# Moving the rounding of two more chunks of h from VectorE to ScalarE in the early blocks of a routed expert network

## The chip, the cores and the metric

The kernel runs on one core of a Trainium2 chip. The metric is the device time of one execution in microseconds, the median of several runs.

## The reference

Each of 32 samples (256 rows of 256 values) is scaled by its condition vector, multiplied by a weight and normalised; the result goes through a mixture of eight experts, of which each row takes the best two, and is added to x.

```python
ys = y * scale
d = rsqrt(einsum('bi,io->bo', ys * ys, weight * weight) + EPS)
z = einsum('bsi,io->bso', x * ys[:, None, :], weight) * d[:, None, :]
logits = einsum('bsd,de->bse', z, Wr) + br
# softmax, top 2 of 8, the two weights normalised: routed
h = relu(einsum('bsd,edh->ebsh', z, W1) + b1)          # 256 -> 1024
expert_out = einsum('ebsh,ehd->ebsd', h, W2) + b2      # 1024 -> 256
out = x + einsum('bse,ebsd->bsd', routed, expert_out)
```

## The kernel before

**Stages.** Stage A computes z and the routing of the first half of the rows. Stage B then works through blocks of rows that share an expert: 14 early blocks (N1 = 14, written out one by one, rows of the first half only), then a loop over further full blocks up to number 38 (NA), then tail blocks of 256 rows. Early and full blocks have 384 rows in three tiles of 128. While the early blocks run, the routing of the second half of the rows is computed in small pieces between their steps (`second_half` on VectorE, ScalarE and TensorE).

**Precision.** TensorE multiplies in fp32r, a rounded form of fp32. Each fp32 operand a is split into a_hi (rounded) and a_lo = a - a_hi, and each product is three matmuls: hi with hi, lo with hi, hi with lo. The split is done for z (z_hi on ScalarE, z_lo on VectorE), for the weights (w_hi on ScalarE, line 783; w_lo on VectorE, line 1396) and for h.

**One block.** The hidden dimension of 1024 is cut into eight chunks c = 0 to 7 of 128. For each chunk:

- `first_product(c)` on TensorE (lines 1653 to 1655): six matmuls of 384 columns into one of two PSUM banks `h_ps[c % 2]`. It waits until ScalarE has read the bank for chunk c - 2.
- ScalarE (`block_of_act`) reads that bank and writes h = relu(. + b1) into one of three SBUF buffers (line 856, counted by `s_relu`). In a chunk that `act_hi` names it first writes h_hi, the rounded relu, from the same bank (line 854, counted by `s_hhi_act`).
- VectorE (`block_of_dve`) makes h_hi from h by a copy (line 1455), unless ScalarE did, and then h_lo = h - h_hi (line 1458, counted by `s_hlo`).
- `second_product(c)` on TensorE (lines 1669 to 1671): nine matmuls of 256 columns, which wait for h_lo.

In the early blocks second products follow three chunks behind. TensorE's order in block b is therefore: first(0), first(1), the six transposes of the next block's rows (line 1631), first(2), first(3), second(0), first(4), second(1), and so on. Between first(1) and first(3) only the transposes and first(2) stand. The wait of a first product is

```python
if not (fresh and c < HP):                 # HP = 2, fresh only in block 0
    pe.wait_ge(s_relu, b * HC + c + 1 - (back(c, HPT) if tail else HP))
```

**ScalarE's order** in an early block: h(0), w_hi of quarter 2, h(1), three copies b2_r (line 864), h(2), w_hi of quarter 3, h_hi(3), h(3), h(4), h(5), w_hi of the next block's quarter 0, h_hi(6), h(6), h_hi(7), h(7), then z_hi and w_hi of the next block's quarter 1. Pieces of the second half's routing stand between some of these in blocks 5 to 10. Instructions of an engine start in this order.

**VectorE's order**: y of the block before, r_cur, then chunk by chunk h_hi (where it is its turn) and h_lo, with w_lo of quarter 2 behind chunk 1, w_lo of quarter 3 behind chunk 3, w_lo of the next block's quarter 0 behind chunk 6, and pieces of the routing behind chunks 2, 4 and 5. first(4) waits for w_lo of quarter 2, first(6) for w_lo of quarter 3.

Of the kernel before, what the change touches and what calls it, by code (L numbers as in the profile page):

```python
# [5 lines left out]
def bass_adaln_moe_ffn(  # L6
# [41 lines left out]
    HC = b1.shape[2]  # L48
# [23 lines left out]
    NHX = 4  # L72
# [22 lines left out]
    N1 = -(-(TOPK * T // 2 - E * (TB - 1)) // TB)  # L95
    NSC1 = N1 * Q
    NB_MIN = NA + -(-(UNITS - Q * NA) // QB)
    ACT_HI = (3, 6, 7)
    TAIL_HI = (3, 6, 7)
    HPT = 3  # L100
    LATE_ACT = (8, 9, 12)
# [13 lines left out]
    with ctx:  # L115
# [3 lines left out]
        def sem(name):  # L119
            return ctx.enter_context(nc.semaphore(name))  # L120
# [258 lines left out]
        s_h2 = sem("s_h2")  # L379
# [12 lines left out]
        def back(c, n=NHP):  # L392

            return n if c >= n else c + 1 + (HC - 1 - c) % n
# [20 lines left out]
        def is_early(b):  # L415
            return isinstance(b, int) and b < N1
# [13 lines left out]
        def act_hi(b, c, tail=False):  # L430
            if tail:
                return c in TAIL_HI
            return isinstance(b, int) and b < N1 - 1 and c in ACT_HI

        def hhi_act(b, c, tail):
            if tail:
                return b * len(TAIL_HI) + (N1 - 1) * len(ACT_HI) - NA * len(TAIL_HI) + TAIL_HI.index(c) + 1
            return b * len(ACT_HI) + ACT_HI.index(c) + 1

        def expert_of(eng, b):  # L440
            if is_early(b):
                eng.wait_ge(s_early, N_EARLY)
                return eng.value_load(early_expert[0:1, b:b + 1], min_val=0, max_val=E - 1)
            if isinstance(b, int):
                eng.wait_ge(s_blocks, N_BLOCKS)
            return eng.value_load(block_expert[0:1, ds(b, 1)], min_val=0, max_val=E - 1)

        def segment_of(eng, b):
            if is_early(b):
                return eng.value_load(early_expert[0:1, b:b + 1], min_val=0, max_val=E - 1)  # L450
            return eng.value_load(block_segment[0:1, ds(b, 1)], min_val=0, max_val=NSEG - 1)
# [250 lines left out]
        def _(act):  # L702
# [76 lines left out]
            def weights_hi(b, k, seg, fresh):  # L779
                act.wait_ge(s_raw[k], seg * 16 + 16)  # L780
                if not fresh:
                    act.wait_ge(s_h2, (b - 1) * HC + (k + 1) * CQ)
                act.activation(w_hi[k][:], raw[k][:], ACT.Copy).then_inc(s_whi, 1)  # L783

            def z_hi_of(b, fresh, width=TB):
                act.wait_ge(s_zt, b + 1)
                if not fresh:
                    act.wait_ge(s_h1, b * HC)
                for c in range(DC):
                    act.activation(z_hi[:, c, 0:width], zt_ps[c][:, 0:width], ACT.Copy).then_inc(s_zhi, 1)  # L790
# [50 lines left out]
            def block_of_act(b, fresh, tail=False):  # L841
                wide = tail or is_early(b)
                width, n_h = (TBT, HPT) if tail else (TB, HP)
                e = expert_of(act, b)
                e_next = expert_of(act, b + 1)
                seg = segment_of(act, b)
                seg_next = segment_of(act, b + 1)
                for c in range(HC):
                    act.wait_ge(s_h1, b * HC + c + 1)
                    if not (fresh and c < NHP):  # L850
                        act.wait_ge(s_hlo, b * HC + c + 1 - back(c))
                    if act_hi(b, c, tail):
                        act.wait_ge(s_h2, b * HC + c + 1 - NHX)
                        act.activation(h_hi[c % NHX][:, 0:width], h_ps[c % n_h][:, 0:width], ACT.Relu,
                                       bias=b1_all[:, ds(e, 1), c]).then_inc(s_hhi_act, 1)
                    act.activation(h[c % NHP][:, 0:width], h_ps[c % n_h][:, 0:width], ACT.Relu,  # L856
                                   bias=b1_all[:, ds(e, 1), c]).then_inc(s_relu, 1)
                    if c == 0:
                        weights_hi(b, 2, seg, fresh)
                    if c == 1:  # L860

                        act.wait_ge(s_rcur, b + 1)
                        for q in range(QB if tail else Q):
                            act.activation(b2_r[:, q, :], b2_all[:, ds(e, 1), :].rearrange("p a d -> p (a d)"),  # L864
                                           ACT.Copy, scale=r_cur[:, q:q + 1]).then_inc(s_b2r, 1)
                    if c == 2:
                        weights_hi(b, 3, seg, fresh)
                    if c == (5 if wide else 4):
                        weights_hi(b + 1, 0, seg_next, False)
                    if c == 5 and not wide:  # L870
                        weights_hi(b + 1, 1, seg_next, False)
                    if is_early(b):
                        second_half(b, c)
                z_hi_of(b + 1, False, width)
                if wide:
                    weights_hi(b + 1, 1, seg_next, False)
# [25 lines left out]
            for b in range(N1):  # L902
                block_of_act(b, b == 0)
            with act.Fori(N1, NA) as b:
                block_of_act(b, False)
            n = blocks_of(act)
            with act.Fori(NA, n) as b:
                block_of_act(b, False, True)
# [837 lines left out]
```

## Time and profile before

| | |
|---|---|
| median of 3 runs | 876.98 us (876.54 to 878.8) |
| profiled execution | 877.7 us, its span 875.9 us |
| TensorE matmuls / weight loads | 842.5 us (96%) / 826.9 us (94%) |
| VectorE | 719.1 us (82%) |
| ScalarE | 563.7 us (64%) |
| GpSimd | 457.5 us (52%) |
| granted TensorE clock, mean | 0.991 |

The span is the time from the first instruction to the last; 1.8 us of the profiled execution lie outside it. Busy shares are means over stages: stage A ends at about 84 us, the early blocks fill the time from there to about 335 us. PE stands for TensorE's matmuls, PEld for its weight loads, DVE for VectorE, ACT for ScalarE. A weight load ahead of each matmul overlaps the matmul before it, so that a gap between weight loads shows best where TensorE stood still.

### The profile page before, as it was taken

The numbers are of one execution on the slowest core, as the hardware profiler recorded it, in microseconds if no ns is written. First come the engines' busy times: TensorE is split into PE (matmuls) and PEld (weight loads), VectorE is DVE, ScalarE is ACT, GpSimd is POOL, SyncE is SP. The second block draws the span as 40 slices with busy tenths as digits, with TensorE's granted clock in tenths as the row PEclk, the third lists the DMA queues.
The fourth block names the chain that finished last, engine by engine and source line by source line (L and its number), as shares of the span: only waits on it lengthen the run. The fifth ranks groups of instructions, "written<-read, shape, count | busy, mean of one in ns | idle before, by whom it ended". The sixth has DMA issues, their size and how long they took to land.

```text
span 875.9 us, 20480 instructions
## 1 busy us (share of the span) xinstructions
PE 842.5 (96%) x6220; PEld 826.9 (94%) x6220; DVE 719.1 (82%) x1423; ACT 563.7 (64%) x1009; POOL 457.5 (52%) x427
## 2 busy tenths in 40 slices
PE   5996999999999999999999999999999999999995
PEld 5975999999999999999999999999999999999995
DVE  3795888899999888788878887888788878888885
ACT  5774666688877665565656655665666566677774
POOL 6973444454444345454545444554555455566563
PEclk9997999999999999999999999999999999999998
DMA  7795856787453354435443543352452524774772
GB/s 241 290 308 190 284 98 171 200 252 191 92 150 79 80 126 96 112 45 132 96 102 48 137 98 91 49 139 53 85 101 57 130 42 115 193 201 115 213 192 24
DMA packets 55097, 118.65 MB, mean 135 GB/s; under 512 B 7344, under 2 KB 33360, under 8 KB 54416
## 3 DMA queue, kind: packets, MB, share of 16 engines
q1 hardware_dynamic: 25040, 69.48, 24.7%
q0 software_dynamic: 25632, 35.96, 24.4%
q10 hardware_dynamic: 4384, 12.71, 4.2%
q8 instruction: 20, 0.33, 0.2%
q14 instruction: 21, 0.17, 0.1%
HBM read 91.34 MB, written 35.17 MB: 144 GB/s over the span
## 4 chain that ended last, share of the span: by engine, by line
PE 76%; DVE 8%; ACT 7%; issue 5%; ACTq 1%; DVEq 1%; DMA 1%; POOL 0%; SPq 0%; POOLq 0%
PE psum L1653 13%; PE psum L1654 12%; PE psum L1655 12%; PE psum L1671 11%; PE psum L1670 11%; PE psum L1669 11%; ACT w_hi L783 3%; ACT h L856 2%; PE psum L1631 2%; DVE w_lo L1396 1%; DVE early_row_hot L1119 1%; PE psum L1544 1%; PE psum L1545 1%; PE psum L1546 1%; DVE y L1426 1%
## 5 line engine op out<-in xcount | busy, mean ns | idle before, releaser
L856 ACT ACTIVATE h<-psum,b_all 128x384 f32<-128x384 f32 (+1 forms) x376 | 208.9, 559 | 232.7 <-PE psum L1655 229.9
L1669 PE MATMUL psum<-w_hi,h_hi 128*128 128x256 f32 x1056 | 296.5, 281 | 1.4 <-DVE h_lo L1458 1.4
L1671 PE MATMUL psum<-w_hi,h_lo 128*128 128x256 f32 x1056 | 295.9, 280 | 0.0
L1670 PE MATMUL psum<-w_lo,h_hi 128*128 128x256 f32 x1056 | 295.9, 280 | 0.0
L1653 PE MATMUL psum<-z_hi,w_hi 128*128 128x384 f32 (+1 forms) x752 | 250.9, 334 | 4.8 <-DVE w_lo L1396 3.0
L1396 DVE TENSOR_TENSOR w_lo<-raw,w_hi 128x1024 fp32r<-128x1024 f32 x190 | 231.8, 1220 | 22.6 <-ACT w_hi L783 22.4
L1654 PE MATMUL psum<-z_lo,w_hi 128*128 128x384 f32 (+1 forms) x752 | 245.4, 326 | 0.0
L1655 PE MATMUL psum<-z_hi,w_lo 128*128 128x384 f32 (+1 forms) x752 | 245.2, 326 | 0.0
L1458 DVE TENSOR_TENSOR h_lo<-h,h_hi 128x384 fp32r<-128x384 f32 (+1 forms) x376 | 200.7, 534 | 25.5 <-ACT h L856 14.8
L783 ACT ACTIVATE w_hi<-raw 128x1024 fp32r<-128x1024 f32 x190 | 200.8, 1057 | 10.6 <-PE psum L1671 9.7
L1669 PEld LDWEIGHTS psum<-w_hi,h_hi 128*128 128x128 f32 x1056 | 199.7, 189 | 3.0 <-issue 2.9
L1671 PEld LDWEIGHTS psum<-w_hi,h_lo 128*128 128x128 f32 x1056 | 200.4, 190 | 0.0
L1670 PEld LDWEIGHTS psum<-w_lo,h_hi 128*128 128x128 f32 x1056 | 199.8, 189 | 0.0
L646 POOL DMA_INDIRECT out<-y,idx_put x91 | 156.0, 1715 | 45.3 <-POOL idx_put L642 25.9
L1455 DVE CAST h_hi<-h 128x384 fp32r<-128x384 f32 (+1 forms) x310 | 113.0, 364 | 71.6 <-ACT h L856 70.6
L1653 PEld LDWEIGHTS psum<-z_hi,w_hi 128*128 128x128 f32 x752 | 142.0, 189 | 8.9 <-ACT h L856 5.6
L1654 PEld LDWEIGHTS psum<-z_lo,w_hi 128*128 128x128 f32 x752 | 141.9, 189 | 0.0
L1655 PEld LDWEIGHTS psum<-z_hi,w_lo 128*128 128x128 f32 x752 | 141.8, 189 | 0.0
L619 POOL DMA_INDIRECT z_row<-z_rows,idx_get x90 | 113.2, 1258 | 44.1 <-POOL idx_get L615 26.8
L604 POOL DMA_INDIRECT z_row<-z_rows,idx_early x42 | 45.4, 1082 | 51.9 <-issue 32.9
L642 POOL COPY idx_put<-idx_all 128x3 int32 (+2 forms) x33 | 6.2, 187 | 120.7 <-DVE y L1426 120.7
L864 ACT ACTIVATE b_r<-b_all,r_cur 128x256 f32 x132 | 57.7, 504 | 0.0
(237 smaller groups left out, 742.2 us busy)
## 6 DMA issues: line engine op xcount, KB each, us to landing
raw<-in_experts SPq DMA_DIRECT2D x96, 512.0 KB, 3.5
x_buf<-in_xT SPq DMA_DIRECT2D x12, 512.0 KB, 8.9
z_rows<-z_all ACTq DMA_DIRECT2D x2, 2112.0 KB, 10.7
d_rep<-d_rows SPq DMA_DIRECT2D x3, 1056.0 KB, 6.7
z_rows<-z_all SPq DMA_DIRECT2D x1, 2112.0 KB, 13.2
z_rows<-z_once SPq DMA_DIRECT2D x1, 2112.0 KB, 14.5
raw<-in_xT SPq DMA_DIRECT2D x4, 512.0 KB, 9.2
out<-y,idx_put POOLq DMA_INDIRECT x91
```

The costliest lines, as they stand in the source:

```text
L619: pool.indirect_dma_start(out=z_row[0][:, q, :], out_offset=None, in_=z_rows, in_offset=bass.IndirectOffsetOnAxis(ap=idx_get[:, q:q + 1], ...
L646: pool.indirect_dma_start(out=out, out_offset=bass.IndirectOffsetOnAxis(ap=idx_put[:, q:q + 1], axis=0), in_=y[0][:, q, :], in_offset=None ...
L783: act.activation(w_hi[k][:], raw[k][:], ACT.Copy).then_inc(s_whi, 1)
L856: act.activation(h[c % NHP][:, 0:width], h_ps[c % n_h][:, 0:width], ACT.Relu, bias=b1_all[:, ds(e, 1), c]).then_inc(s_relu, 1)
L1396: dve.tensor_tensor(out=w_lo[k][:], in0=raw[k][:], in1=w_hi[k][:].bitcast(f32), op=ALU.subtract).then_inc(s_wlo, 1)
L1458: dve.tensor_tensor(out=h_lo[i][:, 0:width], in0=h[c % NHP][:, 0:width], in1=h_hi[i][:, 0:width].bitcast(f32), op=ALU.subtract).then_inc(s ...
L1653: pe.matmul(hp, w1(w_hi, c, dc), z_hi[:, dc, 0:width], start=(dc == 0), stop=False)
L1654: pe.matmul(hp, w1(w_hi, c, dc), z_lo[:, dc, 0:width], start=False, stop=False)
L1655: ins = pe.matmul(hp, w1(w_lo, c, dc), z_hi[:, dc, 0:width], start=False, stop=(dc == DC - 1))
L1669: pe.matmul(yp, hi, w2(w_hi, c), start=(c == 0), stop=False)
L1670: pe.matmul(yp, hi, w2(w_lo, c), start=False, stop=False)
L1671: ins = pe.matmul(yp, lo, w2(w_hi, c), start=False, stop=(c == HC - 1))
```

## The change

`ACT_HI` names the chunks whose h_hi ScalarE makes in blocks 0 to 12. Chunks 1 and 4 are added to 3, 6 and 7. In those two chunks ScalarE issues one more activation, ahead of the one that writes h, and VectorE's copy falls away. Block 13 and all later blocks keep their code; `TAIL_HI` is unchanged. The second edit leaves out a wait of h_hi for a second product that does not exist in block 0 (chunk 1 is now among the chunks below NHX = 4 in which it would be needed).

```diff
-    ACT_HI = (3, 6, 7)
+    ACT_HI = (1, 3, 4, 6, 7)
...
                     if act_hi(b, c, tail):
-                        act.wait_ge(s_h2, b * HC + c + 1 - NHX)
+                        if not (fresh and c < NHX):
+                            act.wait_ge(s_h2, b * HC + c + 1 - NHX)
                         act.activation(h_hi[c % NHX][:, 0:width], h_ps[c % n_h][:, 0:width], ACT.Relu,
                                        bias=b1_all[:, ds(e, 1), c]).then_inc(s_hhi_act, 1)
                     act.activation(h[c % NHP][:, 0:width], h_ps[c % n_h][:, 0:width], ACT.Relu,
```

## Rows read from the trace of the kernel before

**Rows 1.** The page: busy time, and the clock by fortieths of the span.
```profile
PE 842.5 (96%) x6220; PEld 826.9 (94%) x6220; DVE 719.1 (82%) x1423; ACT 563.7 (64%) x1009; POOL 457.5 (52%) x427
...
PEclk9997999999999999999999999999999999999998
```

**Rows 2.** Windows: block 1; stretch, length, busy by engine, clock, DMA share, GB/s.
```profile
104.90:122.20 17.30, 17.30 (x128) 17.27 (x127) 15.03 (x30) 11.48 (x20) 8.34 (x6) 1.00 0.61 143
```

**Rows 3.** Timeline of weight loads, block 1: start, length, instruction; last row is block 2's.
```profile
105.54 0.65 PEld L1631 LDWEIGHTS psum<-ident_r,z_row 128*128 128x128 f32 x6
...
106.95 0.19 PEld L1655 LDWEIGHTS psum<-z_hi,w_lo 128*128 128x128 f32 x1
107.12 0.19 PEld L1653 LDWEIGHTS psum<-z_hi,w_hi 128*128 128x128 f32 x1
...
122.88 0.65 PEld L1631 LDWEIGHTS psum<-ident_r,z_row 128*128 128x128 f32 x6
```

**Rows 4.** Timeline of ScalarE, block 1: h(1), and h_hi(3) with h(3).
```profile
106.41 0.57 ACT L856 ACTIVATE h<-psum,b_all 128x384 f32<-128x384 f32 x1
...
109.49 0.58 ACT L854 ACTIVATE h_hi<-psum,b_all 128x384 fp32r<-128x384 f32 x1
109.95 0.59 ACT L856 ACTIVATE h<-psum,b_all 128x384 f32<-128x384 f32 x1
```

**Rows 5.** Timeline of VectorE: chunk 1 of block 1, two rows of later blocks.
```profile
107.02 0.36 DVE L1455 CAST h_hi<-h 128x384 fp32r<-128x384 f32 x1 [0.41 <-ACT h L856]
107.42 0.56 DVE L1458 TENSOR_TENSOR h_lo<-h,h_hi 128x384 fp32r<-128x384 f32 x1
...
213.66 1.22 DVE L1396 TENSOR_TENSOR w_lo<-raw,w_hi 128x1024 fp32r<-128x1024 f32 x1
...
270.33 0.69 DVE L1188 TENSOR_TENSOR column<-column,mine 128x512 f32<-128x512 f32 x1
```

**Rows 6.** Timeline of weight loads: every one that waited, blocks 1 to 13.
```profile
194.55 0.19 PEld L1653 LDWEIGHTS psum<-z_hi,w_hi 128*128 128x128 f32 x1 [0.51 <-ACT h L856]
201.50 0.19 PEld L1653 LDWEIGHTS psum<-z_hi,w_hi 128*128 128x128 f32 x1 [0.54 <-DVE w_lo L1396]
214.93 0.19 PEld L1653 LDWEIGHTS psum<-z_hi,w_hi 128*128 128x128 f32 x1 [0.19 <-DVE w_lo L1396]
231.47 0.19 PEld L1653 LDWEIGHTS psum<-z_hi,w_hi 128*128 128x128 f32 x1 [0.42 <-ACT h L856]
237.99 0.19 PEld L1653 LDWEIGHTS psum<-z_hi,w_hi 128*128 128x128 f32 x1 [0.19 <-DVE w_lo L1396]
250.21 0.19 PEld L1653 LDWEIGHTS psum<-z_hi,w_hi 128*128 128x128 f32 x1 [0.39 <-ACT h L856]
274.26 0.19 PEld L1653 LDWEIGHTS psum<-z_hi,w_hi 128*128 128x128 f32 x1 [0.37 <-DVE w_lo L1396]
```

**Rows 7.** Timeline of ScalarE: h(1) of blocks 0, 3, 6, 7; h(3), h(4) of block 10.
```profile
88.32 0.58 ACT L856 ACTIVATE h<-psum,b_all 128x384 f32<-128x384 f32 x1 [0.38 <-PE psum L1655]
...
141.08 0.56 ACT L856 ACTIVATE h<-psum,b_all 128x384 f32<-128x384 f32 x1
...
193.93 0.57 ACT L856 ACTIVATE h<-psum,b_all 128x384 f32<-128x384 f32 x1
...
211.80 0.57 ACT L856 ACTIVATE h<-psum,b_all 128x384 f32<-128x384 f32 x1
...
270.33 0.58 ACT L856 ACTIVATE h<-psum,b_all 128x384 f32<-128x384 f32 x1
...
273.16 1.04 ACT L856 ACTIVATE h<-psum,b_all 128x384 f32<-128x384 f32 x2
```

**Rows 8.** Timeline of weight loads: a slow one in block 0, the last before first(3) in blocks 0, 3.
```profile
86.06 0.33 PEld L1654 LDWEIGHTS psum<-z_lo,w_hi 128*128 128x128 f32 x1
...
89.11 0.19 PEld L1655 LDWEIGHTS psum<-z_hi,w_lo 128*128 128x128 f32 x1
...
141.85 0.19 PEld L1655 LDWEIGHTS psum<-z_hi,w_lo 128*128 128x128 f32 x1
```

## The prediction

> **What bounds the kernel now.** I read the page first: matmuls are busy 96% of the span and weight loads 94%, VectorE 82%, ScalarE 64% [rows 1]. That says TensorE sets the pace on the whole, but not whether it does so in blocks 0 to 12, the only ones that change. So next the windows, one per early block. Block 1 is typical: in 17.30 us TensorE is busy for 17.30, VectorE for 15.03 and ScalarE for 11.48 [rows 2]. Third, the timeline of weight loads, for the period of a block: its transposes start at 105.54 in block 1 and at 122.88 in block 2, 17.34 us apart [rows 3]. Fourth, in the same view, every weight load that had to wait, since only there can VectorE's work be on the path that sets the end. After the first product of block 0 there are seven in blocks 0 to 13 [rows 6]: three on ScalarE's h, 0.51 + 0.42 + 0.39 = 1.32 us, and four on VectorE's w_lo, 0.54 + 0.19 + 0.19 + 0.37 = 1.29 us. All lie in blocks 6 to 10, where the second half's routing is squeezed in. In the other early blocks TensorE never waits.
>
> So the early stage is TensorE's, with 2.6 us of waits in it, half of them VectorE's. Taking work from VectorE can give back 1.3 us at most; putting work on ScalarE costs wherever h comes too late for a first product. The question is how near to late h(1) and h(4) are.
>
> **What the change adds.** Two activations per block in 13 blocks, 26 in all, each from a PSUM bank of 384 columns, ahead of the h of the same chunk. In chunk 3 the pair already stands: h_hi starts at 109.49, h at 109.95 [rows 4]. The second of two back-to-back activations starts 0.46 us after the first, so one more delays the h behind it by 0.46. I take 0.46; the bounds are 0.40 (if an h_hi can overlap more) and the 0.58 of one alone.
>
> The Trainium skill, ScalarE: Activation LUTs, What ACT_TABLE_LOAD costs, gives such an activation with a per-partition bias 280 ns and 0.833 ns an element, with an overlap of 93 ns between neighbours. By that, as an estimate, it is 600 - 93 = 507 ns, where the trace shows 0.46 us; with it each delay and so each full stall would be 0.05 us longer and the sum about 0.6 us more. The trace's value stands.
>
> **Chunk 1.** TensorE's program has nothing but transposes and first(2) between first(1) and first(3), and first(3) needs the bank of h(1). In block 1, h(1) runs from 106.41 to 106.98 [rows 4], and first(3)'s first weight load starts at 107.12, unhindered behind one that ends at 107.14 [rows 3]. How fast h releases TensorE is shown in block 6: h(1) ends at 193.93 + 0.57 = 194.50 [rows 7], the load it held back starts at 194.55 [rows 6], so 0.05 us. So h(1) could have let first(3) go at 107.03, a margin of 0.09 us. ScalarE has no gap ahead of h(1): it comes straight behind w_hi of quarter 2, so nothing absorbs the added 0.46. h(1) will end at 107.44 and release at 107.49; weight loads stand still for 107.49 - 107.14 = 0.35 us. Nothing later in the block hides it, since TensorE has no idle time left there.
>
> Other blocks by the same sum. Blocks 2, 4, 5, 11 and 12 have the pattern of block 1, h(1) 0.87 us behind the start of the transposes: 0.35 each. In block 0 h(1) starts at 88.32 [rows 7] and would release at 88.32 + 0.46 + 0.58 + 0.05 = 89.41, against a last weight load that ends at 89.30 [rows 8]: 0.11. In block 3 the ranks' two matmuls stand ahead of the transposes: release at 141.08 + 0.46 + 0.56 + 0.05 = 142.15 against 142.04 [rows 7, 8]: 0.11.
>
> **Chunk 4.** h_hi(4) has room in a plain block: ScalarE has done h(3) when the fourth product's bank is ready, and h(4) is wanted only by first(6), with second(1), first(5) and second(2) between, 24 matmuls. Cost 0; without that cover it would be 0.46 a block. It counts only where routing work sits behind h(3), in block 10.
>
> **What is removed.** Two VectorE copies per block, 0.36 us each in block 1 [rows 5]. In chunk 1 nothing comes of it there: the copy had itself waited 0.41 us for h(1), and h_lo(1) started at 107.42; it will now start at h(1)'s release, 107.49. So VectorE's step behind it, w_lo of quarter 2, is not earlier but 0.07 later, which is covered by TensorE's own 0.35. In chunk 4 VectorE gains some 0.4 us, hidden behind TensorE, as nothing there waits for VectorE.
>
> **Blocks 6 to 10**, where waits exist already, against the old start of the last load that waited:
> - Block 6: h(1) already held first(3) by 0.51; that grows by 0.46. But first(6) was held by w_lo, which started only at VectorE's own pace behind two row_hot instructions. That chain starts with h_lo(1), which starts no earlier than before, as it waits for the later h(1) instead of the copy; I allow 0.06 for what the later h(2) adds. The later TensorE absorbs the rest: +0.06.
> - Block 7: VectorE is behind here, with no wait ahead of its copy. h(1) releases at 211.80 + 0.46 + 0.57 + 0.05 = 212.88, first(3) loses 0.35; but h_lo(1) then starts at once, with no copy ahead of it, and w_lo behind it, which started at 213.66 [rows 5] and held first(4) until 214.93 [rows 6]. first(4) is now wanted at 214.93 - 0.27 + 0.35 = 215.01 (0.27 is what that wait was worth, below) and w_lo, starting by 212.88 + 0.56 = 213.44, ends by 214.66. The wait goes, and the sum is +0.09.
> - Block 8: +0.46 at first(3); the wait at 237.99 on w_lo [rows 6] goes, worth 0.27 (the 0.19 idle and 0.08 by which loads behind a 256-column matmul overlap): +0.19.
> - Block 9: one wait, on h(1): +0.46.
> - Block 10: +0.35 at first(3). Then col_of waits for VectorE's column, which ends at 270.33 + 0.69 = 271.02 [rows 5], while ScalarE had h(3) under way since 270.33 [rows 7] and could have begun at 270.79; of the 0.46 the old gap of about 0.26 takes its part and leaves 0.20. The old h(4) started at 273.16 [rows 7]; now h_hi(4) does at 273.36, h(4) at 273.82, and releases first(6) at 274.45, where w_lo released it at 274.26 [rows 6]: +0.19 in all.
>
> **The sum.** Five blocks like block 1, and block 1: 6 x 0.35 = 2.10. Blocks 0 and 3: 0.22. Blocks 6 to 10: 0.06 + 0.09 + 0.19 + 0.46 + 0.19 = 0.99. Together 3.3 us. After block 12 the code is the same and TensorE-bound, so the rest of the program shifts by this. The profiled execution took 877.7 us, of which 875.9 is span, and would take 881.0; it lies 0.7 above the median of the runs, so the forecast is 876.98 + 3.3 = 880.3 us, 0.38% slower. Bounds: with 0.40 per activation the six plain blocks give 6 x 0.29 and block 9 0.40, in all some 2.7 (879.7); with the full 0.46 lost in 13 blocks and nothing absorbed, 6.0 (883.0).
>
> **Rivals.**
> - *VectorE's relief wins.* If first(3) were not held by h(1) in plain blocks, because its release had more margin than the modelled weight loads show, and ScalarE's lateness in blocks 6 to 9 were covered too, the four w_lo waits would go: -1.3 us, 875.7. For it: VectorE is busy 15 of 17.3 us and did hold TensorE four times. Against: the margin of 0.09 is a fifth of the 0.46 added, and block 6 shows the same wait in action. It decides once h(1)'s margin exceeds 0.46.
> - *The delay mostly fits.* If the margin is truly about 0.3, plain blocks lose 0.15 and blocks 6 to 10 about 0.7: 0.9 + 0.7 = 1.6 us, 878.6, within 0.3%.
> - *No refund.* Blocks 6 to 10 lose their 0.46 in full and the plain ones as well: 883.0. Against it, VectorE's chain there does not depend on h(4) coming early.
> - *The clock falls.* In block 0, after stage A's last gap, weight loads take 0.33 us instead of 0.19 [rows 8], the 1.2 GHz level; about eleven matmuls at 0.32 instead of 0.17 us, 1.6 us an episode. If each of a dozen new stalls brought one, the time would be some 900. Against it, existing stalls of 0.51 and 0.54 us left the clock at 9 tenths or more in all fortieths behind the fourth [rows 1]. The Trainium skill, TensorE: Matmul & The Clock Gate, A second HAM failure mode, speaks of micro-idles between groups of matmuls that make the clock oscillate; the trace does not bear it out for gaps of this size.
>
> **How the numbers follow.** The forecast case 0.66, the delay mostly fits 0.18, no refund 0.08, relief wins 0.06, clock 0.02. 0.3% is 2.6 us, about what a measurement of this kernel can tell from no change. The forecast case reaches slightly below that edge (0.10 of its 0.66). So slower 0.66, same 0.30 and faster 0.04 (a relief larger than the one worked out). The range goes from the case that mostly fits, 878.3, to most of the no-refund case, 882.6. The likeliest case alone spans 879.5 to 881.2.
>
> **What would show it.** In the timeline of weight loads, blocks 1, 2, 4, 5, 11 and 12 should each show one load of line 1653 idle for about 0.35 us on ScalarE's h, and the transposes 17.7 us apart. The total of waits on h should be near 5 us with 12 or 13 entries (1.32 before), and w_lo's should fall from 1.29 to some 0.3 to 0.6. VectorE's copies of line 1455 should number 26 fewer, ScalarE's h_hi 26 more. The prediction is wrong if first(3) starts on time in block 1, or if waits on another engine's work appear behind chunk 4.

## The result, and the profile after

The changed kernel takes 881.48 us (median of 8 runs, 879.77 to 882.01) against 877.08 us before: ratio 1.0044, with an interval of 1.0035 to 1.0052, so 3.9 us or 0.44% slower. The forecast was 880.3. Profiled execution against profiled execution the span grew from 875.9 to 879.8 us. Of these 3.9 us, 0.30 lie ahead of block 0, where the code is the same, and 3.6 in blocks 0 to 12.

From ScalarE's activations on, line numbers are one higher than before (h is line 857, the first product starts at line 1654). The page, answering to [rows 1]:

```profile
span 879.8 us, 20482 instructions
PE 844.3 (96%) x6220; PEld 826.1 (94%) x6220; DVE 710.8 (81%) x1397; ACT 575.6 (65%) x1035; POOL 461.9 (53%) x427
...
PEclk9997999999999999999999999999999999999998
```

The same matmuls, 26 VectorE instructions fewer (1423 to 1397, 8.3 us less busy) and 26 on ScalarE more (1009 to 1035, 11.9 us more). The shares say nothing of the price. The waits of weight loads from 84 to 335 us do (total, times, longest):

```profile
PEld psum L1654 <- ACT h L857: 5.9, 12, 1.0
PEld psum L1654 <- issue: 1.5, 1, 1.5
PEld psum L1654 <- DVE w_lo L1397: 0.7, 2, 0.3
PEld psum L1671 <- issue: 0.3, 1, 0.3
```

Before, h held TensorE three times for 1.32 us and w_lo four times for 1.29 us [rows 6]. Now h does so twelve times for 5.9 us and w_lo twice for 0.7. The sum went from 2.6 to 6.6 us. The 1.5 us on "issue" stand at the start of block 0 in both traces. So does one of 0.16 us at the ranks' matmuls in block 3, which [rows 6] leave out. The forecast expected near 5 us on h, though the waits of its own terms add up to 5.7.

Block 1, weight loads around first(3), answering to [rows 3]:

```profile
106.09 0.66 PEld L1632 LDWEIGHTS psum<-ident_r,z_row 128*128 128x128 f32 x6
...
107.50 0.19 PEld L1656 LDWEIGHTS psum<-z_hi,w_lo 128*128 128x128 f32 x1
108.06 0.19 PEld L1654 LDWEIGHTS psum<-z_hi,w_hi 128*128 128x128 f32 x1 [0.37 <-ACT h L857]
108.16 0.19 PEld L1655 LDWEIGHTS psum<-z_lo,w_hi 128*128 128x128 f32 x1
```

ScalarE and VectorE in the same block, answering to [rows 4, 5]:

```profile
106.96 0.57 ACT L855 ACTIVATE h_hi<-psum,b_all 128x384 fp32r<-128x384 f32 x1
107.42 0.58 ACT L857 ACTIVATE h<-psum,b_all 128x384 f32<-128x384 f32 x1
...
108.04 0.56 DVE L1459 TENSOR_TENSOR h_lo<-h,h_hi 128x384 fp32r<-128x384 f32 x1 [0.88 <-ACT h L857]
108.51 1.22 DVE L1397 TENSOR_TENSOR w_lo<-raw,w_hi 128x1024 fp32r<-128x1024 f32 x1
```

h(1) starts 0.46 us behind h_hi(1), ends at 108.00, and TensorE's load follows at 108.06, 0.37 us after the load before it ended. VectorE, relieved of its copy, waits for the same h(1), now for 0.88 us. The window of block 1, answering to [rows 2], shows that neither of the other engines was busy all the time: of 17.65 us VectorE is busy for 14.36 and ScalarE for 12.43.

```profile
106.10:123.75 17.65, 17.60 (x128) 17.24 (x128) 14.36 (x27) 12.43 (x24) 8.53 (x7) 1.00 0.53 128
```

The loads that waited on h or w_lo in blocks 6 to 10, answering to [rows 6] (each of the blocks 0, 2, 4, 5, 11 and 12 has one more on h, 0.28 us in block 0 and 0.35 to 0.37 in the others):

```profile
196.77 0.19 PEld L1654 LDWEIGHTS psum<-z_hi,w_hi 128*128 128x128 f32 x1 [0.98 <-ACT h L857]
203.42 0.19 PEld L1654 LDWEIGHTS psum<-z_hi,w_hi 128*128 128x128 f32 x1 [0.33 <-DVE w_lo L1397]
214.82 0.19 PEld L1654 LDWEIGHTS psum<-z_hi,w_hi 128*128 128x128 f32 x1 [0.36 <-ACT h L857]
234.07 0.19 PEld L1654 LDWEIGHTS psum<-z_hi,w_hi 128*128 128x128 f32 x1 [0.89 <-ACT h L857]
253.02 0.19 PEld L1654 LDWEIGHTS psum<-z_hi,w_hi 128*128 128x128 f32 x1 [0.86 <-ACT h L857]
270.68 0.19 PEld L1654 LDWEIGHTS psum<-z_hi,w_hi 128*128 128x128 f32 x1 [0.37 <-ACT h L857]
277.33 0.19 PEld L1654 LDWEIGHTS psum<-z_hi,w_hi 128*128 128x128 f32 x1 [0.32 <-DVE w_lo L1397]
```

In blocks 6, 8 and 9 the old wait on h grew by 0.47 each. In blocks 7 and 8 the waits on w_lo are gone.

How much each block grew, from the starts of successive transposes (block 0 from its first weight load, 84.65 before and 84.95 after), beside the working of the forecast:

| block | 0 | 1 | 2 | 3 | 4 | 5 | 6 | 7 | 8 | 9 | 10 | 11 | 12 | sum |
|---|---|---|---|---|---|---|---|---|---|---|---|---|---|---|
| forecast, us | 0.11 | 0.35 | 0.35 | 0.11 | 0.35 | 0.35 | 0.06 | 0.09 | 0.19 | 0.46 | 0.19 | 0.35 | 0.35 | 3.3 |
| measured, us | 0.25 | 0.31 | 0.34 | 0.02 | 0.28 | 0.25 | 0.18 | 0.21 | 0.20 | 0.46 | 0.44 | 0.32 | 0.33 | 3.6 |

Block 13, whose code is the same, is as long as before to 0.01 us (transposes of block 14 at 337.30 before and 341.18 after). The rest of the program is only shifted.

### The profile page after: what moved, and what is told of

It reads as the page before. It is cut to its first block, busy times and chain, and to the rows that moved or that the text cites. A ratio compares the mean times of both kernels' runs of the same rounds, so it can differ in the third digit from the quotient of the medians.

```text
span 879.8 us, 20482 instructions
## 1 busy us (share of the span) xinstructions
PE 844.3 (96%) x6220; PEld 826.1 (94%) x6220; DVE 710.8 (81%) x1397; ACT 575.6 (65%) x1035; POOL 461.9 (53%) x427
## 4 chain that ended last, share of the span: by engine, by line
PE 74%; ACT 9%; DVE 9%; issue 5%; ACTq 1%; DVEq 1%; DMA 1%; POOL 0%; SPq 0%; POOLq 0%
PE psum L1654 12%; PE psum L1671 11%; PE psum L1672 11%; PE psum L1670 11%; PE psum L1655 11%; PE psum L1656 11%; ACT w_hi L783 3%; ACT h L857 2%; PE psum L1632 2%; ACT h_hi L855 1%; DVE y L1427 1%; DVE h_lo L1459 1%; DVE w_lo L1397 1%; DVE early_row_hot L1120 1%; PE psum L1545 1%
## 5 line engine op out<-in xcount | busy, mean ns | idle before, releaser
L1456 DVE CAST h_hi<-h 128x384 fp32r<-128x384 f32 (+1 forms) x284 | 102.3, 360 | 67.0 <-ACT h L857 63.2
L604 POOL DMA_INDIRECT z_row<-z_rows,idx_early x42 | 48.7, 1160 | 52.8 <-issue 33.7
L855 ACT ACTIVATE h_hi<-psum,b_all 128x384 fp32r<-128x384 f32 (+1 forms) x92 | 50.8, 552 | 31.0 <-PE psum L1656 21.8
```

## The experiments

Each was timed beside the kernel before. The stage figure, from block 1's transposes to block 14's in one profiled execution, leaves out block 0. That block is 1.2 us shorter in the traces of runs 5, 9 and 11 than in the trace before: all its weight loads take 0.19 us there, where ten take 0.33 before. A small difference of the ratio can come from this too. The stage is 231.76 us before and 235.09 after.

| kernel | ratio to before, interval | stage, us | against before |
|---|---|---|---|
| the change | 1.0044, 1.0035 to 1.0052 | 235.09 | +3.33 |
| 1: chunk 1 alone | 1.0038, 1.0025 to 1.0051 | 234.97 | +3.21 |
| 2: chunk 4 alone | 1.0009, 0.9999 to 1.0018 | 232.32 | +0.56 |
| 3: added, not removed | 1.0049, 1.0036 to 1.0061 | 236.02 | +4.26 |
| 4: chunks 2 and 4 | 1.0014, 1.0005 to 1.0023 | 232.02 | +0.26 |
| 5: chunk 2 alone | 1.0006, 0.9996 to 1.0015 | 231.32 | -0.44 |
| 6: w_hi behind h(1) | 1.0071, 1.0058 to 1.0085 | 237.86 | +6.10 |
| 7: and b2_r behind h(2) | 1.0040, 1.0026 to 1.0053 | 234.33 | +2.57 |
| 8: rounded from h | 1.0035, 1.0023 to 1.0048 | 234.17 | +2.41 |
| 9: and w_lo behind chunk 0 | 1.0021, 1.0012 to 1.0029 | 233.32 | +1.56 |
| 10: w_lo ahead of routing | 1.0010, 1.0001 to 1.0018 | 232.52 | +0.76 |
| 11: and pieces behind chunk 4 | 0.9997, 0.9988 to 1.0006 | 231.26 | -0.50 |
| 12: the pieces alone | 0.9996, 0.9987 to 1.0006 | 231.17 | -0.59 |

### 1 and 2: one chunk at a time

```diff
-    ACT_HI = (1, 3, 4, 6, 7)
+    ACT_HI = (1, 3, 6, 7)      # run 1
+    ACT_HI = (3, 4, 6, 7)      # run 2
```

> The changed kernel without chunk 4: ScalarE rounds h in chunks 1, 3, 6, 7 of blocks 0 to 12. Theory (the whole price is h(1) behind h_hi(1), which holds first(3)): nearly all of the measured +4.4 us stays, +3.3 to +4.5 us over the kernel before, and plain blocks show the same idle of 0.35 to 0.37 us at one weight load. Rival (the load on ScalarE as such, in either chunk, costs): about half, near +2 us.

> The changed kernel without chunk 1: ScalarE rounds h in chunks 3, 4, 6, 7. Theory: h(4) has time, so no new waits in plain blocks; in blocks 6 to 10 VectorE's copy that is saved stands behind w_lo of quarter 3, so the w_lo waits of 0.54, 0.19, 0.19 and 0.37 us stay: -0.5 to +0.5 us against the kernel before. Rival (load as such): near +2 us. Rival (VectorE's relief has a price of its own): -1 us or less.

Chunk 1 alone has all of it: 1.0038, 3.3 us, and a stage 3.21 us longer of the change's 3.33, with the same wait in block 1:

```profile
107.64 0.19 PEld L1654 LDWEIGHTS psum<-z_hi,w_hi 128*128 128x128 f32 x1 [0.37 <-ACT h L857]
```

Chunk 4 alone gives 1.0009, whose interval just reaches no change: a little above what was expected. In its stage of +0.56 there are one new wait on w_lo of 0.21 us in block 8 and one of 0.30 us in block 7 that the trace gives to nothing; no plain block (1, 2, 4, 5, 11 and 12) has a wait. The rival of a price for each added activation, +2 us for either, falls.

### 3: the added work without the relief

```diff
+                    if c == 1 and isinstance(b, int) and b < N1 - 1:
+                        if not fresh:
+                            act.wait_ge(s_h2, b * HC + c + 1 - NHX)
+                        act.activation(h_hi[c % NHX][:, 0:width], h_ps[c % n_h][:, 0:width], ACT.Relu,
+                                       bias=b1_all[:, ds(e, 1), c])
                     act.activation(h[c % NHP][:, 0:width], h_ps[c % n_h][:, 0:width], ACT.Relu,
```

> The kernel before, with one more activation in chunk 1 of blocks 0 to 12: ScalarE writes h_hi(1), and VectorE's copy writes it again. So the cost of the change in chunk 1 without its relief for VectorE. Theory: plain blocks lose the same 0.36 us; blocks 6 to 10, where the relief refunded about 0.3 us in blocks 7 and 8, lose more than in the changed kernel: +4.0 to +5.5 us against the kernel before. Rival (the relief is worth more than the trace shows): over +6 us.

+4.3 us by the ratio, as expected. The stage is 1.05 us longer than with chunk 1 alone, and that is what the saved copy of chunk 1 is worth. The waits on w_lo in this run:

```profile
203.79 0.19 PEld L1658 LDWEIGHTS psum<-z_hi,w_hi 128*128 128x128 f32 x1 [0.55 <-DVE w_lo L1401]
...
241.10 0.19 PEld L1658 LDWEIGHTS psum<-z_hi,w_hi 128*128 128x128 f32 x1 [0.18 <-DVE w_lo L1401]
...
278.32 0.19 PEld L1658 LDWEIGHTS psum<-z_hi,w_hi 128*128 128x128 f32 x1 [0.46 <-DVE w_lo L1401]
```

With chunk 1 alone they were 0.33, none and 0.23 us. Block 6 is 0.24 us longer than there, block 8 0.28 and block 10 0.37. Block 7, where a refund by the relief was expected too, is only 0.03 longer: its old wait on w_lo stays away without the relief, absorbed by the later first(3).

### 4 and 5: the same work in chunk 2

```diff
-    ACT_HI = (1, 3, 4, 6, 7)
+    ACT_HI = (2, 3, 4, 6, 7)   # run 4
+    ACT_HI = (2, 3, 6, 7)      # run 5
```

> The same added work as in the changed kernel, but in chunks 2 and 4 instead of 1 and 4. Theory (place decides): h(2) is late by 0.46 us too, but first(4) wants it some 0.5 us after it was ready before, so plain blocks show no wait; the saved copy of chunk 2 stands ahead of w_lo of quarter 3 and shortens its waits in blocks 6, 8 and 10 by up to 0.3 us each. Against the kernel before -1.0 to +0.5 us. Rival (two more activations on ScalarE cost wherever they stand): +3 us or more.

> ScalarE rounds h in chunks 2, 3, 6, 7. Theory: as with chunks 2 and 4, without what chunk 4 adds: -1.0 to +0.3 us against the kernel before. If this is below both kernels, it is the version to keep.

Run 4 adds as many activations as the change and costs 1.2 us by the ratio instead of 3.9. No plain block has a wait. The stage, +0.26 us, lies inside the expected range and the ratio above it. Part of that is not in the blocks: in all its runs 2.2 to 2.3 us lie outside the span, where the kernel before has 1.8. What the rest of the difference is, the one trace does not show. Inside the stage some 0.4 us are gained in blocks 6 and 7, and blocks 9 and 10 give back 0.6: in blocks 6, 8 and 9 the later ScalarE now holds first(5), and in block 10 first(6) is later than before.

```profile
198.33 0.19 PEld L1654 LDWEIGHTS psum<-z_hi,w_hi 128*128 128x128 f32 x1 [0.26 <-ACT h L857]
...
234.72 0.19 PEld L1654 LDWEIGHTS psum<-z_hi,w_hi 128*128 128x128 f32 x1 [0.21 <-ACT h L857]
...
273.66 0.19 PEld L1654 LDWEIGHTS psum<-z_hi,w_hi 128*128 128x128 f32 x1 [0.65 <-DVE w_lo L1397]
```

Run 5 has only the first kind, the waits of first(5), and one of 0.36 us in block 0; its waits on w_lo are down from 1.29 us to 0.2. Its time can't be told from the kernel before.

### 6 and 7: w_hi out of h(1)'s way

```diff
-                    if c == 0:
+                    if c == (1 if act_hi(b, 1) and not tail else 0):      # runs 6 and 7
                         weights_hi(b, 2, seg, fresh)
-                    if c == 1:
+                    if c == (2 if act_hi(b, 1) and not tail else 1):      # run 7 alone
                         act.wait_ge(s_rcur, b + 1)
```

> All five chunks as in the changed kernel, but in blocks 0 to 12 ScalarE makes w_hi of quarter 2 behind h(1) instead of between h(0) and h(1). Theory: h(1) is then done some 0.5 us ahead of first(3) and the 0.36 us waits vanish; w_lo of quarter 2 begins with w_hi's end, about 0.1 us later than in the kernel before, just in time for first(4). Expected -1 to +1 us against the kernel before, blocks 1 to 5 within 0.1 us of 17.34. If the price were ScalarE's added load and not the place of h(1), it would stay near +4.4 us.

This took 6.2 us more than the kernel before, where -1 to +1 was expected. first(3) did start on time in blocks 1 to 12 (in block 0 it still waited 0.52 us), but the time came back, and more, at first(4). ScalarE, VectorE and weight loads of block 2:

```profile
123.37 0.58 ACT L857 ACTIVATE h<-psum,b_all 128x384 f32<-128x384 f32 x1 [2.60 <-PE psum L1656]
124.41 0.58 ACT L855 ACTIVATE h_hi<-psum,b_all 128x384 fp32r<-128x384 f32 x1 [0.46 <-PE psum L1656]
...
127.50 0.57 ACT L857 ACTIVATE h<-psum,b_all 128x384 f32<-128x384 f32 x1
...
126.44 1.23 DVE L1397 TENSOR_TENSOR w_lo<-raw,w_hi 128x1024 fp32r<-128x1024 f32 x1 [0.39 <-ACT w_hi L783]
...
128.19 0.19 PEld L1654 LDWEIGHTS psum<-z_hi,w_hi 128*128 128x128 f32 x1 [0.45 <-DVE w_lo L1397]
```

With w_hi gone from between h(0) and h(1), ScalarE idles 0.46 us for first(1), and all that follows is later by as much. The load of first(4) is put down to w_lo, but w_lo ended at 127.67; h(2) ended at 128.07, 0.12 ahead of the load. Run 7 tested that reading.

> The kernel with w_hi of quarter 2 behind h(1), and now b2_r too moved, behind h(2). That run was 7 us slower than the kernel before, with 0.43 to 0.45 us at first(4) in each block, which the trace puts on w_lo or on nothing; my reading is that h(2) released it, since ScalarE idled 0.46 us for h1(1) where w_hi stood before. With b2_r's 1.2 us out of its way h(2) is early, and only w_lo of quarter 2 is left, which ends 0.2 us late. Theory: 0.2 us or a little more a block, +2 to +4.5 us. Rival (w_lo released it all along, as the view says): still +7 us.

1.0040, 3.5 us, inside the range; the stage fell from 237.86 to 234.33 us by moving three activations for which TensorE has no wait. w_lo of quarter 2 ends as long behind the transposes as in run 6, 3.73 us against 3.74, and first(4) now starts at 3.78 instead of 4.26. So h(2) had been the releaser in run 6.

What is left is not where the expectation had it, so that its number is right by luck. w_lo makes first(4) only 0.05 us late. The rest, about 0.22 us a block, stands at first(5), released by h(3), which now comes behind b2_r, w_hi and h_hi(3). VectorE's w_lo, ScalarE's h(3) and the first loads of first(4) and first(5), block 2:

```profile
125.34 1.22 DVE L1397 TENSOR_TENSOR w_lo<-raw,w_hi 128x1024 fp32r<-128x1024 f32 x1 [0.39 <-ACT w_hi L783]
...
126.61 0.19 PEld L1654 LDWEIGHTS psum<-z_hi,w_hi 128*128 128x128 f32 x1
...
128.28 0.59 ACT L857 ACTIVATE h<-psum,b_all 128x384 f32<-128x384 f32 x1
...
128.92 0.19 PEld L1654 LDWEIGHTS psum<-z_hi,w_hi 128*128 128x128 f32 x1
```

h(3) ends at 128.87. First(5) started 5.82 us behind the transposes before and starts 6.09 behind them here. In both runs the 0.46 us between h(0) and h_hi(1), which w_hi had filled, stand empty, and both are slower than the kernel before.

### 8 and 9: the bank released first

```diff
-                    if act_hi(b, c, tail):
+                    if act_hi(b, c, tail) and c != 1:
...
+                    if c == 1 and act_hi(b, c, tail):      # behind h
+                        if not fresh:
+                            act.wait_ge(s_h2, b * HC + c + 1 - NHX)
+                        act.wait_ge(s_relu, b * HC + c + 1)
+                        act.activation(h_hi[c % NHX][:, 0:width], h[c % NHP][:, 0:width],
+                                       ACT.Copy).then_inc(s_hhi_act, 1)
...
-                    if c == (0 if tail else 1):            # run 9 alone, VectorE
+                    if c == (0 if tail or (is_early(b) and b < N1 - 1) else 1):
                         weights_lo(b, 2)
```

> The changed kernel, with chunk 1's rounding on ScalarE behind h(1) and read from h instead of from the PSUM bank: the same number of activations, the same relief for VectorE, but the bank is free 0.46 us earlier. Theory: the 0.36 us waits on h(1) vanish; h(2) is now late by 0.46 us plus what ScalarE's wait for its own h(1) takes, about 0.1, and is just in time for first(4) or 0.1 late: 0 to +1.5 us against the kernel before. Rival (ScalarE's load is the price): +4.4 us as before.

The waits on h(1) vanished from the plain blocks, yet it took 3.1 us by the ratio, 1.6 above the expected range. Another wait took their place. Block 2, ScalarE and VectorE:

```profile
124.65 0.53 ACT L865 ACTIVATE h_hi<-h 128x384 fp32r<-128x384 f32 x1
...
125.30 0.56 DVE L1465 TENSOR_TENSOR h_lo<-h,h_hi 128x384 fp32r<-128x384 f32 x1 [1.13 <-ACT h_hi L865]
125.78 1.22 DVE L1403 TENSOR_TENSOR w_lo<-raw,w_hi 128x1024 fp32r<-128x1024 f32 x1
```

h_lo(1) comes later, and w_lo of quarter 2 stands behind it in VectorE's queue though it needs nothing of it. It ends at 127.00, and first(4), due 3.74 us behind the transposes at 123.12 (as 109.28 stood to 105.54 before), wanted it by 126.86; its load stands at 127.05.

> The kernel that rounds chunk 1 from h behind h(1) was 3.7 us slower than the kernel before, where 0 to 1.5 were expected: plain blocks are 17.51 us instead of 17.34. My reading: VectorE waits 1.13 us for that later h_hi(1), and w_lo of quarter 2 stands behind it in its queue and reaches first(4) 0.17 us late. Here, in blocks 0 to 12, VectorE makes w_lo of quarter 2 behind chunk 0, in that gap. Theory: plain blocks are back at 17.34 to 17.40 us, -0.5 to +1.0 us against the kernel before, with five chunks rounded by ScalarE. Rival (a general price of ScalarE's load): +3.7 us as before.

1.0021: 1.8 us instead of 3.1. Plain blocks are 17.41 us apart instead of 17.51, against 17.34 before. The range was missed by 0.8 us. The 0.07 us of a plain block stand at first(4), which h(2) now releases (it ends at 124.75 in block 2, the load starts at 124.86). Blocks 6 to 10 have 1.14 of the stage's 1.56 us: h(2) and h(3), behind ScalarE's pieces of routing, hold first(4) and first(5) in blocks 6, 8 and 9, and h(4), behind col_of, holds first(6) in block 10. So all five chunks can be rounded by ScalarE for 1.8 us instead of 3.9, but not for nothing.

### 10, 11 and 12: the old waits, by order alone

```diff
-                    if c == 3:                                # runs 10 and 11
+                    if c == (2 if is_early(b) else 3):
                         weights_lo(b, 3)
...
-                if b == 6 and c in (0, 2):                    # runs 11 and 12
-                    hot_scaled(1, c // 2)
+                if b == 6 and c in (4, 5):
+                    hot_scaled(1, c - 4)
...
-                if b in (8, 9) and c in (0, 2):
-                    g = HG + (b - 8) * BG + c
+                if b in (8, 9) and c in (4, 5):
+                    g = HG + (b - 8) * BG + 2 * (c - 4)
```

Here `ACT_HI` is (3, 6, 7), as before.

> The kernel before, with three chunks on ScalarE, but in the early blocks VectorE makes w_lo of quarter 3 behind h_lo(2), ahead of the routing pieces, instead of behind h_lo(3). Theory: the w_lo waits of first(6) in blocks 6, 8 and 10, 0.54 + 0.19 + 0.37 us, go by order alone, without taking any work off VectorE: -1.3 us to -0.6 us. Rival (VectorE is short of time there, whatever the order): the waits move to another instruction, 0 or slower.

Slower by 0.9 us, where 0.6 to 1.3 less were expected. The waits of first(6) in blocks 6 and 8 and of first(4) in block 7 went, but VectorE's later routing pieces now hold second products in blocks 5, 6 and 7, and in block 10 ScalarE's col_of waits for a column that VectorE makes 1.1 us later in the block, with h(4) behind it:

```profile
189.18 0.19 PEld L1669 LDWEIGHTS psum<-w_hi,h_hi 128*128 128x128 f32 x1 [0.47 <-DVE h_lo L1458]
...
271.49 2.18 ACT L776 ACTIVATE col_of<-column 128x512 bf16<-128x512 f32 x2 [1.27 <-DVE column L1188]
...
274.25 0.19 PEld L1653 LDWEIGHTS psum<-z_hi,w_hi 128*128 128x128 f32 x1 [1.05 <-issue]
```

> As the kernel with w_lo of quarter 3 ahead of the routing, and ScalarE's pieces of routing in blocks 6, 8 and 9 (hot_scaled, partial_of) moved from behind h(0) and h(2) to behind h(4) and h(5). Theory: they made h(1) late, so its three waits of 0.51, 0.42 and 0.39 us go too: -1.8 to -2.6 us against the kernel before, faster than both kernels.

> The kernel before, with only ScalarE's pieces of routing in blocks 6, 8 and 9 moved from behind h(0) and h(2) to behind h(4) and h(5); w_lo of quarter 3 stays where it was. In the run with both moves the three waits on h went, 1.32 us, and the move of w_lo had cost 0.8 us by itself, as its waits came back on h_lo of chunk 7's block end and at first(6). Theory: -1.0 to -1.5 us, below both kernels; the w_lo waits of 0.54, 0.19, 0.19 and 0.37 us stay or shorten by little. Rival (the pieces, wherever they stand, cost ScalarE's time): 0.

In run 11 the stage is 1.26 us shorter than in run 10, the size of the three waits on h that went. Against the kernel before only 0.50 us are gained, where 1.8 to 2.6 were expected. In run 12, expected at -1.0 to -1.5 us, these waits are gone too, and yet the stage is only 0.59 us shorter than before:

```profile
PEld psum L1653 <- DVE w_lo L1396: 1.6, 4, 0.6
PEld psum L1653 <- issue: 1.5, 1, 1.5
PEld psum L1671 <- issue: 0.4, 1, 0.4
```

TensorE, no longer held by h(1), reaches first(4) earlier and waits there for w_lo instead, 0.58 us in block 8; 0.36 us more stand in block 7 without a releaser. Neither kernel can be told from the one before; none beats it.

## Why the prediction was right

**The place of the price.** The step that carried the forecast was chunk 1: nothing but transposes and first(2) between first(1) and first(3), a margin of 0.09 us, 0.46 us added. Block 1 shows it (wait 0.37, forecast 0.35), chunk 1 alone has 3.21 of the 3.33 us, and chunk 2 with chunk 4, the same number of activations, has 0.26. Run 8, with as many activations but the bank released first, has no wait on h(1) in plain blocks.

**Its size.** 3.3 us were forecast, 3.6 came in blocks 0 to 12 and 3.9 by the ratio. The blocks' own sum is in part luck: the plain blocks and block 3 came out 0.36 us below their terms, blocks 0, 6, 7 and 10 some 0.63 above theirs. Plain blocks grew by 0.25 to 0.34 instead of 0.35: the wait is as long as forecast, but behind a wait the next load follows after 0.10 us (108.06 to 108.16) where it took 0.17, so a part comes back. Block 3's 0.11 shrank to 0.02.

**Blocks 6 to 10.** Blocks 8 and 9 came out as worked out, 0.20 and 0.46. In block 8 the wait on w_lo went because of the saved copy: in run 3, without the relief, it is back and the block grows by 0.47. Block 9 had no wait to absorb anything. In block 6 a part of the 0.46 was absorbed, also by the relief (0.42 in run 3, 0.18 with it); the 0.06 allowed for the later h(2) was too small, as VectorE's copy h_hi(2) started 0.10 us later in the block and took 0.43 us instead of 0.35.

In block 7 the working held up to first(4), 0.05 us late where 0.09 was forecast. Behind it stands a gap of 0.27 on "issue" inside a second product, which the forecast did not have. In its place a short wait of second(7) is gone, which the view before does not list (h_lo(7) ended at 226.32, the load started at 226.38 where it was due at 226.16), so that without the gap the block would have been shorter than before.

The term for block 10 was mis-sized, 0.44 for 0.19. The chain through col_of and h(4) is the forecast one: h_hi(4) starts 7.42 us behind the transposes, 7.44 by the forecast. But first(6) started 0.27 us later than its old place, released by h(4) about 0.12 us after it ended and not 0.05, and about 0.16 us more stand at second(7), which waits for h_lo(7); that step the forecast left out:

```profile
276.61 1.08 ACT L857 ACTIVATE h<-psum,b_all 128x384 f32<-128x384 f32 x2
...
283.77 0.56 DVE L1459 TENSOR_TENSOR h_lo<-h,h_hi 128x384 fp32r<-128x384 f32 x1 [1.60 <-ACT h L857]
...
284.38 0.19 PEld L1670 LDWEIGHTS psum<-w_hi,h_hi 128*128 128x128 f32 x1
```

**Block 0** waited 0.28 us instead of 0.11. The slow weight loads began one load earlier than in the trace before, in first(0), so that all of ScalarE is later by 0.14: h_hi(1) started 3.81 us behind the block's first load (88.76 against 84.95), where h(1) had started 3.67 behind it (88.32 against 84.65).

**Chunk 4** was costed at nothing in plain blocks, and no run shows a wait there. It counts in block 10, as forecast: that block grew by 0.13 us with chunk 1 alone and by 0.44 with both. Its relief shows no gain: chunk 1 alone is as fast as both chunks within the interval.

**The relief for VectorE** was costed in blocks 6 to 8 alone. The run with the work added but not removed puts it at 1.05 us in all, near the 0.93 by which the terms of blocks 6 to 8 stay below what their first(3) loses. That the sums agree is luck: block 7's part needs no relief, and block 10's 0.37 was not in the forecast. In the plain blocks the relief could not be a gain, as h_lo(1) waits for the same h(1) that was made late.

**The rivals.** That the delay mostly fits needed a margin of 0.3; it was 0.09, too little also for VectorE's relief to win, which needed more than 0.46. No refund would have been 6 us. The clock stayed up: the fortieths read as before, and from 90 to 335 us the granted clock is 1.00 in both traces, though fourteen weight loads in this stretch stood still for 0.27 to 0.98 us after the change. The forecast read the fortieths as 9 tenths or more behind the fourth; the last one, at the end of the program, is 8, before and after.

## What to carry to other kernels

Before moving work to an engine that is idle a third of the time, look at what its next instruction releases and how soon that is wanted: here 0.46 us in front of one instruction made TensorE wait some 0.36 us and the block some 0.3 us longer each time, while the same 0.46 us one chunk later cost nothing in the plain blocks. Of the orders tried here the old one is best for the instruction that frees a bank for TensorE: ahead of it stands a filler that is just as long as the gap; both moving the filler away (+6.1 us of stage) and adding to it (+3.3 us) lost. After each reorder read the queue behind the delayed instruction: four of the orders tried here (runs 6, 8, 10 and 12) removed waits at which they aimed and gave all or part of the time back at w_lo, h(2) or h_lo, which stood behind them.

## What the runs showed of the hardware that was not expected

The trace's releaser can be wrong where a load waits for two things: in run 6 the load at 128.19 is put down to w_lo, which had ended 0.52 us earlier; h(2), over for 0.12 us, was the one, as run 7 confirmed. In block 10 after the change the load at 277.33 is put down to w_lo in the same way, 0.20 us after it ended.

TensorE's load follows the h that releases it after 0.05 us at first(3), and after 0.11 to 0.12 us at first(4) in runs 6 and 9 and first(6) of block 10 after the change. These products wait for w_lo as well; where w_lo comes last it releases them after 0.05 us (127.00 to 127.05 in run 8). That the second wait makes the difference is not shown.

In six of the fourteen traces (the change, runs 1, 2, 3, 6 and 12) one weight load in block 7 stands still for 0.27 to 0.37 us with no releaser, 12.8 to 13.6 us behind the transposes. It is the fourth to seventh of the nine loads of second(4), between which the program has no wait; the kernel before and seven others lack it. What causes it stays open. It is a tenth of the change's effect.
